# The half tiles of a mixture of experts moved to the middle of the expert stage, and eight result slots in place of four

## What is computed

```
router_logits = einsum('bsd,de->bse', layernorm(x), gate_w)      # 8 experts
top_logits, top_idx = top_k(router_logits, 2)
top_w = softmax(top_logits)
h = silu(einsum('bsd,edf->ebsf', layernorm(x), w1))              # 256 -> 512
y = einsum('ebsf,efd->ebsd', h, w2)                              # 512 -> 256
out = x + sum over the two chosen experts of top_w * y
```

## Time and profile before

| | |
|---|---|
| median of 3 runs | 716.13 us (714.78 to 716.4) |
| profiled execution | 715.26 us, span 713.5 us, granted clock 0.988 |
| busy share of PE, PEld, DVE, ACT, POOL | 90%, 74%, 73%, 63%, 68% |
| first scatter-add of the expert stage | 505.2 us after the span's start |
| scatter-adds in all (L527) | 71, mean 1,592 ns on POOL |

### The profile page before, as it was taken

One profiled execution on the slowest core, in us unless ns is written; L12 is line 12 of the kernel. 1 busy time (PEld: TensorE's weight loads), 2 busy tenths in 40 slices (PEclk: granted clock), 3 DMA queues, 4 the chain that ended last, 5 costly groups with the idle time before them and its releaser, 6 DMA issues. The chain is left out here.

```text
span 713.5 us, 22010 instructions
## 1 busy us (share of the span) xinstructions
PE 639.0 (90%) x7612; PEld 528.3 (74%) x7613; DVE 519.7 (73%) x1226; ACT 446.3 (63%) x768; POOL 483.3 (68%) x577
## 2 busy tenths in 40 slices
PE   6627799999999999999999999979999999999871
PEld 2215587788788888788788778757888888888751
DVE  3964679988988998898898898986577644445431
ACT  1436787778778778778778877854464454454330
POOL 3024645878878877977877887875677676556744
PEclk9999899999999999999999999999999999999997
DMA  8921111112111121111211211203769989655630
GB/s 263 322 79 21 32 34 52 48 45 68 47 55 57 47 62 50 59 53 48 75 36 48 80 32 48 78 16 77 119 124 136 133 119 139 92 82 87 86 48 6
DMA packets 87259, 55.31 MB, mean 78 GB/s; under 512 B 60784, under 2 KB 81520, under 8 KB 87216
## 3 DMA queue, kind: packets, MB, share of 16 engines
q1 hardware_dynamic: 73840, 37.41, 22.2%
q0 software_dynamic: 13376, 17.33, 13.4%
HBM read 20.27 MB, written 24.85 MB: 63 GB/s over the span
## 5 line engine op out<-in xcount | busy, mean ns | idle before, releaser
L527 POOL DMA_INDIRECT out_x<-pt_s,token_of x71 | 113.0, 1592 | 23.4 <-issue 21.4
L782 DVE TENSOR_TENSOR wq_s<-wk_s,wq_s 128x512 f16<-128x512 f32 (+1 forms) x78 | 51.5, 664 | 78.6 <-ACT wq_s L603 78.5
L598 ACT ACTIVATE wk_s<-ps 128x512 f32<-128x512 f32 (+1 forms) x78 | 43.5, 557 | 102.9 <-PE ps L1600 99.0
L1600 PE MATMUL ps<-ffnw,wq_s 128*128 x852 | 100.1, 273 | 6.3 <-DVE wq_s L782 4.8
L1600 PE MATMUL ps<-q_s,ffnw 128*128 128x256 f16 (+1 forms) x936 | 103.3, 264 | 2.1 <-issue 1.6
L959 POOL TENSOR_TENSOR prob<-prob,mx 128x1168 f32<-128x1168 f32 x64 | 77.6, 1233 | 37.6 <-DVE mx L1401 37.5
L1600 PEld LDWEIGHTS ps<-q_s,ffnw 128*128 x936 | 86.0, 98 | 15.2 <-issue 4.6
L1600 PEld LDWEIGHTS ps<-ffnw,wq_s 128*128 128x128 f16 x852 | 81.7, 98 | 19.8 <-issue 9.8
L1600 PE MATMUL ps<-wo_s,ot_s 128*128 128x256 f16 x768 | 89.4, 273 | 2.8 <-DVE ot_s L1338 2.8
L1600 PE MATMUL ps<-xt_s,wq_s 128*128 128x256 f16 x768 | 89.9, 279 | 1.9 <-DVE xt_s L1338 1.9
L1600 PEld LDWEIGHTS ps<-xt_s,wq_s 128*128 128x128 f16 x768 | 76.5, 100 | 13.0 <-issue 1.9
(11 more groups left out here) (232 smaller groups left out, 1176.0 us busy)
## 6 DMA issues: line engine op xcount, KB each, us to landing
wstage<-in_ffn_w SPq DMA_DIRECT2D x16, 512.0 KB, 3.6
x_sb<-in_x SPq DMA_DIRECT2D x4, 1024.0 KB, 10.8
out_x<-x_sb SPq DMA_DIRECT2D x16, 256.0 KB, 2.2
rows_dram<-wstage SPq DMA_DIRECT2D x8, 264.0 KB
out_x<-pt_s,token_of POOLq DMA_INDIRECT x71
pt_s<-in_wq SPq DMA_DIRECT2D x2, 512.0 KB, 4.4
pt_s<-in_wo SPq DMA_DIRECT2D x2, 512.0 KB, 8.4
rows_dram<-row_words,slot_i POOLq DMA_INDIRECT x64, 2.5
```

Of the source, the lines that this page charges most:

```text
L527: pool.indirect_dma_start(out_rows, bass.IndirectOffsetOnAxis(ap=token_of[:, j % UNROLL, c:c + 1], axis=0), y_sb[:, j % UNROLL, c, :], Non ...
L598: act.activation(h32[:, half, 0:2 * n], h_ps(t, j, half)[:, 0:2 * n], ACT.Silu, scale=1 / WSCALE).then_inc(silu_done, 1)
L782: dve.tensor_tensor(hs[:, j % 2, 1, 2 * half:2 * half + 2, 0:n], h32[:, half, 0:2 * n].rearrange("p (f n) -> p f n", f=2), hs[:, j % 2, 0, ...
L1600: last = pe.matmul(o, lhs(a, n), rhs(c, n), start=(i == 0), stop=(i == len(steps) - 1))
```

## The change

The half tiles become tiles 20 to 26 and the twelve late full tiles become 27 to 38 (LATE0 = EARLY + NH = 27). `subs`, the tables and the counts of landed additions follow. `y_sb`, `wt` and `token_of` get YS = 8 slots, and `weights_in` waits for the tile eight back, from tile 8 on. Both the first half tile and the first late full tile wait for all earlier additions without the table. The tiles from 16 on are written out, without a loop. A further small table (`earlier_late`) is made on POOL. The numbers of tiles, of matmuls and of scatter-adds stay.

```
+LATE0 = EARLY + NH
+YS = 8
-            return 1 if isinstance(t, int) and t >= FULL else SUB
+            return 1 if isinstance(t, int) and EARLY <= t < LATE0 else SUB
...
-            split, loops = (EARLY - UNROLL) // UNROLL, (FULL - UNROLL) // UNROLL
-            for r in range(1, split):
+            for r in range(1, EARLY // UNROLL - 1):
                 with eng.Fori(r, r + 1) as i:
                     for j in range(UNROLL):
-                        step(i * UNROLL + j, j, False)
+                        step(i * UNROLL + j, r * UNROLL + j, False)
                         then(r * UNROLL + j)
             between()
-            with eng.Fori(split, loops) as i:
-                for j in range(UNROLL):
-                    step(i * UNROLL + j, j, True)
-            for t in range(loops * UNROLL, NT):
+            for t in range(EARLY - UNROLL, NT):
                 step(t, t, True)
...
-                if isinstance(t, int) and t == FULL:
-                    started, before_expert = False, landed(FULL - 1)
+                if isinstance(t, int) and t in (EARLY, LATE0):
+                    started, before_expert = False, landed(t - 1)
...
-                        out_rows, bass.IndirectOffsetOnAxis(ap=token_of[:, j % UNROLL, c:c + 1], axis=0),
-                        y_sb[:, j % UNROLL, c, :], None, bounds_check=TOKENS - 1, oob_is_err=False,
+                        out_rows, bass.IndirectOffsetOnAxis(ap=token_of[:, j % YS, c:c + 1], axis=0),
+                        y_sb[:, j % YS, c, :], None, bounds_check=TOKENS - 1, oob_is_err=False,
...
-                if not (isinstance(t, int) and t < UNROLL):
-                    dve.wait_ge(added[j % 2], landed_before(t, j, UNROLL))
+                if j >= YS:
+                    dve.wait_ge(added[j % 2], landed_before(t, j, YS))
...
-            pool.iota(earlier_half[:], [[16, NH // 2], [0, 2]], base=landed(FULL - 1), channel_multiplier=0,
+            pool.iota(earlier_half[:], [[16, NH // 2], [0, 2]], base=landed(EARLY - 1), channel_multiplier=0,
                       allow_small_or_imprecise_dtypes=True)
-            pool.iota(earlier[:], [[16 * SUB, FULL // 2], [16 * SUB, 2]], base=-16 * SUB, channel_multiplier=0,
+            pool.iota(earlier_late[:], [[16, LATE - 1]], base=landed(LATE0 - 2), channel_multiplier=0,
+                      allow_small_or_imprecise_dtypes=True)
+            pool.iota(earlier[:], [[16 * SUB, EARLY // 2], [16 * SUB, 2]], base=-16 * SUB, channel_multiplier=0,
                       allow_small_or_imprecise_dtypes=True).then_inc(pad_made, 1)
```

More of the change, by code:

```diff
@@ L175, in build @@
         e_of = sb("e_of", [P, EARLY], F32)
-        wt = sb("wt", [P, UNROLL, SUB], F32)
-        token_of = sb("token_of", [P, UNROLL, SUB], I32)
+        wt = sb("wt", [P, YS, SUB], F32)
+        token_of = sb("token_of", [P, YS, SUB], I32)
         table = sb("table", [1, 2, EARLY], I32)
@@ L183, in build @@
         e_of_all = sb("e_of_all", [P, NT], F32)
-        earlier = sb("earlier", [1, FULL], F32)
+        earlier = sb("earlier", [1, EARLY], F32)
+        earlier_late = sb("earlier_late", [1, LATE - 1], F32)
         earlier_half = sb("earlier_half", [1, NH - 1], F32)
@@ L431, in subs @@
         def subs(t):
-            return 1 if isinstance(t, int) and t >= FULL else SUB
+            return 1 if isinstance(t, int) and EARLY <= t < LATE0 else SUB
         def landed(t):
             return sum(16 * subs(i) for i in range(t % 2, t + 1, 2))
+        assert all(landed(LATE0 + k - 2) == landed(LATE0 - 2) + 16 * k for k in range(LATE - 1))
+        assert all(landed(EARLY + k - 2) == landed(EARLY - 1) + 16 * (k // 2) for k in range(NH - 1))
         def run_tiles(eng, step, between, then=lambda t: None):
@@ L661, in early_table @@
                 dve.wait_ge(pad_made, 3)
-                adds(adds_early[:], earlier[:, 0:EARLY], RT, EARLY, start_of[0:1, :]).then_inc(tab_done, 1)
+                adds(adds_early[:], earlier[:], RT, EARLY, start_of[0:1, :]).then_inc(tab_done, 1)
                 link(dve.tensor_tensor(used[:], tiles_e[:], ends[:], ALU.subtract))
@@ L733, in full_experts @@
             def full_experts():
-                experts_of(EARLY, LATE)
+                experts_of(LATE0, LATE)
             def full_table():
-                table_of(EARLY, LATE, RT, rest)
-                link(adds(adds_all[:, EARLY:FULL], earlier[:, EARLY:FULL], RT, LATE, all_starts[0:1, 0:LATE]))
+                table_of(LATE0, LATE, RT, rest)
+                link(dve.tensor_tensor(new_expert[:, 0:LATE], all_starts[0:1, 0:LATE], tnum[0:1, 0:LATE], ALU.is_equal))
+                link(dve.scalar_tensor_tensor(
+                    out=adds_all[:, LATE0 + 1:NT], in0=new_expert[:, 1:LATE], scalar=float(16 * SUB),
+                    in1=earlier_late[:], op0=ALU.mult, op1=ALU.add))
             def half_rows():
@@ L753, in half_table @@
                 dve.scalar_tensor_tensor(
[L754 removed]
+                    out=adds_all[:, EARLY + 1:LATE0], in0=new_expert[:, 1:NH], scalar=16.0, in1=earlier_half[:],
                     op0=ALU.mult, op1=ALU.add).then_inc(tab_done, 1)
@@ L763, in weights_in @@
             def weights_in(t, j, whole):
-                if not (isinstance(t, int) and t < UNROLL):
-                    dve.wait_ge(added[j % 2], landed_before(t, j, UNROLL))
+                if j >= YS:
+                    dve.wait_ge(added[j % 2], landed_before(t, j, YS))
                 dve.wait_ge(meta_in[j % UNROLL], slot_wait(t, j))
                 n = subs(t)
-                dve.tensor_copy(token_of[:, j % UNROLL, 0:n], meta_words[:, j % UNROLL, 0:n, 0])
+                dve.tensor_copy(token_of[:, j % YS, 0:n], meta_words[:, j % UNROLL, 0:n, 0])
                 meta = meta_words[:, j % UNROLL, 0:n].bitcast(F32)
-                dve.scalar_tensor_tensor(out=wt[:, j % UNROLL, 0:n], in0=meta[:, :, 1], scalar=(e_of_all if whole else e_of)[:, bass.ds(t, 1)],
+                dve.scalar_tensor_tensor(out=wt[:, j % YS, 0:n], in0=meta[:, :, 1], scalar=(e_of_all if whole else e_of)[:, bass.ds(t, 1)],
                                          in1=meta[:, :, 2], op0=ALU.is_equal, op1=ALU.mult).then_inc(wt_done, 1)
                 dve.wait_ge(wt_done, 2 * t + 1)
-                dve.tensor_tensor(wt[:, j % UNROLL, 0:n], wt[:, j % UNROLL, 0:n], meta[:, :, 3], ALU.add
+                dve.tensor_tensor(wt[:, j % YS, 0:n], wt[:, j % YS, 0:n], meta[:, :, 3], ALU.add
                                   ).then_inc(wt_done, 1)
```

12 lines of the change are left out of this document (6 added, 6 removed).

## The result

The changed kernel took 721.06 us (median of seven runs, 718.0 to 723.3) against 716.17 us for the kernel before, beside it on the same chip (seven runs, 714.4 to 717.93). The ratio is 1.0066, with a 95% interval of 1.004 to 1.0092: slower, by 4.9 us. The same kernel in a later series gave 719.26 us and 1.005 (1.0026 to 1.0074). The forecast was 715.6 us, range 713.0 to 717.8; the result lies outside it.

What follows compares the result with a forecast made beforehand. POOL's chain of scatter-adds waiting for landings was taken as the bound. Its pieces, reordered, moved the span from 713.5 to 713.0 us; that -0.5 on the 716.13 median gave 715.6 us, range 713.0 to 717.8.

Steps and rivals of the forecast that it cites:

- What bounds the kernel: Expert stage: POOL's chain of scatter-adds waiting for earlier ones to land, 46.2 us of waits; PE a close second pace.
- the old end: Kernel before, from 617.92 us: late full tiles 66.75, half tiles with rows 17.86, padding and the end 10.97 us.
- Eight slots and straight code at nothing: Slots worth nothing, bounds 0 to 0.5 us, off the path; code without the loop might give PE up to 1 us.
- the pieces are the same in another order: From tile 20 on: scatter-adds and expert switches keep their number, so moved pieces keep their sizes; new end 713.0 us.
- Tile 20's gate: First half tile in the new order: gate opens at 617.92 us as before, since tile 19's chain is untouched.
- The padding: Three padding tiles moved to the middle: 7.45 us from tile 24's gate to tile 27's at 643.7.
- The late tiles: Late full tiles, gate 27 to gate 38: 58.36 us, taken over unchanged, with tile 38's gate at 702.1.
- The surcharge of the half tiles: Four half tiles beside a busier DMA: +0.13 us each, +0.5 in all; bounds 0 to +0.32 each.
- The end: After tile 38's last issue at 704.9: landing 4.4 us later at 709.3, then 3.66 us, so 713.0.
- rival 1: End counted from POOL's last issue, 6.19 us later, not the landing: span -2.2 us, time 713.9; chance 0.33.
- Rival 2: PE takes over at tile 27 if half tiles take 5.24 us: +2.0 us, time 718.1; chance 0.13.
- Rival 3: Half tiles' scatters share the DMA, 3.4 us in place of 0.5: +2.4 us, time 718.5; chance 0.04.

Runs made afterwards that it cites:

- experiment 1: The kernel before, in the old order with four slots, but the tiles from 16 on written out in place of the loop: 716.7 us, ratio 1.0008.
- experiment 2: The kernel before, in the old order, with the tiles from 16 on written out and eight result slots: 717.36 us, ratio 1.0014.
- experiment 3: The changed kernel with four slots in place of eight: 721.31 us, ratio 1.0074 to the kernel before.
- experiment 4: The changed kernel unchanged, traced and timed once more: 719.26 us, ratio 1.005 to the kernel before.
- experiment 9: Experiment 1 with SP holding each late load until POOL opens the gate of the tile before: 717.37 us, ratio 0.9999 to the kernel before.
- experiment 14: Old order, written out, without the transposed loads of tiles 24 to 30 (full tiles there): 716.18 us, ratio 0.9997 to the kernel before.
- experiment 5: The kernel before with SP loading only a quarter of each tile's transposed rows from tile 20 on: 713.83 us, ratio 0.997.
- experiment 7: The kernel before without scatter-adds for the three padding tiles, their gates kept: 712.19 us, ratio 0.9936.
- experiment 11: The kernel before with one more DVE instruction, so padding tiles don't count as a new expert and don't wait: 713.62 us, ratio 0.9958.
- experiment 10: The changed kernel with SP holding late loads until a small POOL instruction behind the scatter-adds has run: 719.63 us, ratio 1.0043 to the kernel before.
- experiment 8: The changed kernel without scatter-adds for its three padding tiles, their gates kept: 718.39 us, ratio 1.0022 to the kernel before.
- experiment 6: The changed kernel with SP loading only a quarter of each tile's transposed rows from tile 20 on: 717.77 us, ratio 1.0025 to the kernel before.
- experiment 12: The changed kernel with one more DVE instruction, so padding tiles don't count as a new expert: 719.92 us, ratio 1.0049 to the kernel before.
- experiment 13: The changed kernel without the transposed loads of tiles 24 to 30 (three half, four full): 719.65 us, ratio 1.0066 to the kernel before.

## Why the prediction was wrong

**What bounds the kernel: right.** The chain of scatter-adds bounds both kernels, and experiments 1 to 4 show that its order is what costs. One slip in "the old end" changes nothing in the sum: the 3.66 us run to the end of the span at 713.5, not to 713.30.

**Eight slots and straight code at nothing: right in the medians.** 1.0008 with straight code and 1.0014 with both, each within 0.4% by its interval. DVE's wait for a slot is gone and nothing came of it. The sum did not count the four further instruction fetches of the straight code; one of them falls beside tile 17, as the next paragraph says.

**The failed step: "the pieces are the same in another order".** The sum moved pieces and kept their sizes; the sizes changed with what ran beside them, as far as the causes are known. Four terms were mis-sized.
- Tile 20's gate, taken as untouched. In the changed kernel's trace it came 2.4 us later, 1.95 of it in one step, tile 17 to 18 (8.50 against 6.55). It varies: counted from tile 15's gate, tile 20's came 25.0 to 25.3 us later in before, 1, 2, 3 and 4, and 27.5 in this execution of the changed kernel, but also 26.9 in the old order of experiments 9 and 14. In the four traces with the loop (before, 5, 7, 11) no 16 KB fetch falls beside tile 17 and the step to 18 takes 6.55 to 6.8 us. In the twelve of written-out code one begins 1.7 to 4.1 us behind tile 17's second issue, and the step takes 6.6 to 8.7: 7.6 or more in two of four of the old order and in five of eight of the new. So it goes with the straight code rather than with the order, as far as these traces tell.
- The padding, 7.45 from an idle DMA; measured 8.7 to 9.1. In the changed kernel 0.9 of the 1.3 is the load of a full tile beside the last scatter-add (experiment 10). With a quarter of the bytes the padding took 7.5.
- The late tiles, 58.36 from gate 27 to 38; measured 60.3, 60.3, 61.8. One us of it is tile 27's issue, 1.71 us behind its gate (646.75 to 648.46) where 0.73 is usual. It was 1.70 to 1.71 in all seven traces of the new order with padding scatter-adds ahead, and 0.71 in the one without (experiment 8). Whether these scatter-adds cause it, or where the code lies, stays open. Without it they took 59.3 to 60.8, which is about what executions of the old order differ by: these tiles took 58.4 before, 60.4 and 60.6 in experiments 1 and 2, and 58.7 in experiments 9 and 11. The prediction had named a change of this spacing as the thing that would make it wrong.
- The surcharge of the half tiles, +0.5, bounds 0 to 1.3: about 0 in the changed kernel's first trace, +2.5 in experiments 3 and 4 (and +0.4 and +1.5 in 8 and 10). It was bounded by full tiles' second scatter-adds, behind which a late first one is hidden (experiment 9); a half tile has one scatter-add alone, with nothing to hide behind.

**The end: the likeliest value was wrong, rival 1 right.** It was 6.35 us from the last issue, with a landing of 3.8 hidden in it (experiments 7 and 11). This went in the kernel's favour by 1.7 us; without it the miss would have been larger. The Trainium skill (GPSIMD Engine Reference, section Instruction dispatch) ties a POOL instruction's end to its cores and to no landing; these runs agree as far as the landing goes, though no run shows what the 4.4 to 4.6 us of the DRAIN behind it are spent on.

**Rival 2, PE at tile 27.** Not in the changed kernel: DVE had finished tile 27's rows at 643.9 (the line below), forecast 643.1, and the gate opened at 646.75, released by a DMA.

```profile
643.03 0.88 DVE L797 TENSOR_SCALAR pt_s<-ps,wt 128x256 f32<-128x256 f32 x2 [0.53 <-PE ps L1607]
```

But only because the chain was late: where the padding was cheaper (experiments 6, 8 and 12) DVE released that gate. Both sums put it at 643.7, 0.2 us ahead of these rows, so PE would have cost them 0.3 us or so, not the 2.0 of rival 2.

**Rival 3, half tiles that share the DMA.** Given 4%, priced at +3.4 for the half tiles. A mechanism of its kind occurred in experiments 3 and 4 (+2.5 us, in part perhaps the fetches) and in the padding of the changed kernel. I argued against it with lone full tiles at a DMA share of 0.60, the wrong witness. The Trainium skill (DMA: Bandwidth & Descriptors, section Queues, rings and completion order) has each DMA engine alternate between the queues with work. The traces look less even: where a load's packets began first, the scatter-add's began up to 1.8 us late (3.93 us after the issue in place of 2.13).

**What stays open.** The medians differ by 3.0 (experiment 4) to 4.9 us. The spans of the three traces of each order differ by 3.2 in the mean, 2.4 of it behind tile 20's gate: half tiles +1.6, late tiles +1.0, the swap of the padding for the old switch and end -0.25 (9.0 + 9.1 against 7.4 + 10.9 in the means); the rest lies ahead of that gate or in executions that weren't profiled. Executions differ by more than this before the change begins to act: tile 15's gate came between 592.6 and 597.4 us in the 16 traces. How much of the half tiles' part is the row loads, and how much the 16 KB instruction fetches that began 1.7 and 2.6 us behind two of the slow scatter-adds (tile 22 in experiments 4 and 3), wasn't separated: experiment 13 took the loads away in a single trace, and its median did not follow.

## What to carry to other kernels

Before moving a short piece of a serial chain from a quiet stretch into a busy one, size it by a row from the busy stretch of the same shape: a lone transfer shows a delay that a pair hides. Where there is no such row, as here, the upper bound of that term is open, and the range should say so. Look at what the piece covered at its old place and what it covers at the new one; here the padding cost as much in the middle as the switch and the tail that it replaced, and PE stood close behind it. And where an engine's last instruction starts the program's end, make that instruction come earlier: letting the padding go without waiting gave 3 us in the old order with one small DVE instruction.

## What the hardware showed that I had not expected

POOL's DRAIN ends 4.4 to 4.6 us after the end of POOL's last instruction, whether that is a scatter-add in flight or a 0.2 us addition (experiment 7). A scatter-add's packets mostly begin 2.1 us after its issue, and up to 3.9 us after it where a transposed load begins within 0.8 us of it. Its landing usually follows 0.5 us behind its last packet; in seven of the eight steps where it took 1.0 us or more, a 16 KB instruction fetch ran within 0.1 us of that packet's end.
